# A fused graph network and LSTM kernel: first layer reassociated, first loads reordered, edge tables moved into LSTM pass 2

## The reference, cut to what matters

```python
# x (128 batches, 128 nodes, 128 features), adj (128, 128)
h = relu(einsum('ts,bsh->bth', adj, x @ Wg0 + bg0))
h = relu(einsum('ts,bsh->bth', adj, h @ Wg1 + bg1))
for p in 1, 2, 3, 4:                   # an LSTM over windows of p nodes;
    h[last node of each window] = lstm_last(Wih[p-1], Whh[p-1], ..., windows of p)
x = layernorm(x + h)
x = layernorm(x + edge_attention(x, W_lin, W_val, a, W_out, adj, src, dst))   # 256 edges
```

## Time and profile before

| | us |
|---|---|
| median of 3 runs | 902.23 (901.87 to 903.23) |
| the profiled execution | 902.41 |
| its span in the trace | 900.6 |
| PE busy | 873.2 (97%) |
| DVE busy | 695.8 (77%) |
| ACT busy | 611.2 (68%) |
| POOL busy | 175.7 (20%) |

### The profile page before, as it was taken

The page is one execution under the profiler, slowest core; times in us unless marked ns, Lnnn a source line. Parts: engine busy times, 40 slices in busy tenths (PEclk is TensorE's granted clock), DMA queues, the critical chain, the costliest instruction groups (busy, mean ns, idle before and its releaser), DMA issues.

```text
span 900.6 us, 15429 instructions
## 1 busy us (share of the span) xinstructions
PE 873.2 (97%) x5411; PEld 759.2 (84%) x5411; DVE 695.8 (77%) x1570; ACT 611.2 (68%) x1115; POOL 175.7 (20%) x498
## 2 busy tenths in 40 slices
PE   6999999998999999999999999999998999999996
PEld 6888888886787779999998887878887888888885
DVE  5777777777778777777777676767987887887886
ACT  1777777776777676677667666666787676776354
POOL 0000000000000000000000010003465465566765
PEclk9999999999999999999999999999999999999999
DMA  4212221001000000000000067677155011110222
GB/s 112 78 43 57 71 60 47 25 1 47 1 1 0 1 1 1 1 1 1 1 2 0 1 146 175 147 170 158 48 116 119 14 36 37 36 37 24 58 62 82
DMA packets 43275, 45.44 MB, mean 50 GB/s; under 512 B 2592, under 2 KB 40128, under 8 KB 40128
## 3 DMA queue, kind: packets, MB, share of 16 engines
q1 hardware_dynamic: 39520, 27.47, 10.6%
q0 software_dynamic: 2304, 16.78, 9.2%
q10 hardware_dynamic: 1376, 0.22, 0.2%
HBM read 19.29 MB, written 8.39 MB: 31 GB/s over the span
## 4 chain that ended last, share of the span: by engine, by line
PE 85%; DVE 8%; ACT 3%; issue 2%; POOL 0%; POOLq 0%; DVEq 0%; ACTq 0%
PE psum L446 8%; PE psum L448 8%; PE psum L447 8%; PE psum L464 6%; PE psum L460 6%; PE psum L461 6%; PE psum L1102 6%; PE psum L1178 6%; PE psum L364 3%; PE psum L382 3%; PE psum L392 3%; PE psum L1191 2%; PE psum L1158 2%; PE psum L355 2%; PE psum L354 2%
## 5 line engine op out<-in xcount | busy, mean ns | idle before, releaser
L564 ACT ACTIVATE work<-psum,bias 128x512 f32<-128x512 f32 (+1 forms) x408 | 233.1, 622 | 29.2 <-PE psum L464 28.6
L446 PE MATMUL psum<-hT_hi,w_hi 128*128 128x512 f32 (+1 forms) x408 | 148.8, 365 | 3.3 <-ACT work L564 2.6
L448 PE MATMUL psum<-hT_hi,w_lo 128*128 128x512 f32 (+1 forms) x408 | 147.3, 361 | 0.0
L447 PE MATMUL psum<-hT_lo,w_hi 128*128 128x512 f32 (+1 forms) x408 | 147.3, 361 | 0.0
L548 ACT ACTIVATE work<-work 128x512 f32<-128x512 f32 (+1 forms) x112 | 63.8, 570 | 102.3 <-DVE work L819 70.9
L1010 POOL DMA_DIRECT2D hT_lo<-hT_hi x8 | 7.3, 916 | 556.9 <-DVE hT_lo L794 537.7
L828 DVE TENSOR_TENSOR work<-work 128x512 f32<-128x512 f32 (+1 forms) x111 | 67.8, 611 | 54.1 <-ACT work L548 54.1
L460 PE MATMUL psum<-hs_hi,w_hi 128*128 128x512 f32 (+1 forms) x288 | 103.8, 360 | 0.8 <-DVE hs_hi L792 0.6
L464 PE MATMUL psum<-hs_lo,w_hi 128*128 128x512 f32 (+1 forms) x288 | 104.3, 362 | 0.0
L461 PE MATMUL psum<-hs_hi,w_lo 128*128 128x512 f32 (+1 forms) x288 | 103.2, 358 | 0.0
L446 PEld LDWEIGHTS psum<-hT_hi,w_hi 128*128 128x128 f32 x408 | 76.8, 188 | 17.4 <-ACT work L564 5.4
(11 more groups left out here) (206 smaller groups left out, 1861.0 us busy)
## 6 DMA issues: line engine op xcount, KB each, us to landing
work<-x SPq DMA_DIRECT2D x32, 256.0 KB, 3.0
x_stage<-x_by_feature SPq DMA_DIRECT2D x8, 1024.0 KB, 5.6
hT_lo<-hT_hi POOLq DMA_DIRECT2D x8, 1024.0 KB, 9.7
hT_lo<-x_stage POOLq DMA_DIRECT2D x8, 1024.0 KB, 7.0
out<-x_kept SPq DMA_DIRECT2D x31, 256.0 KB, 2.3
work<-L_gnn_Wih SPq DMA_DIRECT2D x4, 256.0 KB, 3.5
work<-L_gnn_Whh SPq DMA_DIRECT2D x3, 256.0 KB, 3.0
out<-x_kept SPq DMA_DIRECT2D x2, 128.0 KB, 2.3
```

What stands on the lines that cost most here:

```text
L446: pe.matmul(out, w_hi[:, w, g, :], xh, start=True, stop=False)
L447: pe.matmul(out, w_hi[:, w, g, :], xl, start=False, stop=False)
L448: mm = pe.matmul(out, w_lo[:, w, g, :], xh, start=False, stop=(t == 0))
L564: op = act.activation(gate[s][g][:, 0:ph.width], psum[:, 4 * s + g, 0:ph.width], ACT.Tanh if g == G else ACT.Sigmoid, bias=bias[:, b:b + 1])
```

## The change

Eight things are done.

1. First layer. Per tile PE computes `xw` = x times Wg0 first (four fp32 products, from a host-side layout `xb` with features on the partitions), ACT writes its high part, DVE a new low part (`xw_ready`), and `h1` = adj times xw is three F32R matmuls of 512 columns instead of four fp32 products. `adjT` is split once for it.
2. First loads. x is loaded from `xb` in rows of 2048 bytes. SP issues x tile 0, waits until it has landed, and only then issues tiles 1 and 2, the weights, the edge numbers and `a`. ACT issues Wg0, adj and the bias first, then runs a one-column activation, then the rest.
3. PE runs five small matmuls on `ones` before adj is there, and one after its transpose.
4. `degrees` moves behind slot 0, `rank_rows` behind slot 1, the LSTM biases get their own transposition behind slot 3.
5. The attention's weights are centred after slot 6, turned after slot 7 and copied after slot 8.
6. The edge tables leave pass 1: on DVE they go before items 1, 3, 5, 7, 8, 12, 13, 15, 16, 17, 19 and 21 of pass 2, on PE before items 8, 12 and 16 of pass 2 (`sort_cols`, `sort_rows` in F32R, `adjacent`, in bank F) and item 6 of pass 3 (`log_to_rows`), on ACT the logarithm goes behind item 2 of pass 3.
7. In the last slots of pass 1 ACT reads gate O before it does tanh, DVE does the cell product earlier, and in slot 36 PE does the I and G products of pass 2's item 0 ahead of the last O product.
8. `region_free` also waits for `log_ready`.

```diff
 # run_sync
-        sp.dma_start(adj_sb[:, :], adj).then_inc(S["adj_loaded"], 16)
         load_x(0)
-        sp.dma_start(wg0[:, :], Wg0).then_inc(S["wg0_loaded"], 16)
-        sp.dma_start(edge_row_i[:, :], ...)
+        sp.wait_ge(x_loaded[0], 16)
         load_x(1)
+        load_x(2)
         load_piece(0)
         for j, w in enumerate((W_lin, W_val, W_out)):
             sp.dma_start(w_raw[1][:, j, :], w).then_inc(raw_loaded[1], 16)
-        load_x(2)
+        sp.dma_start(edge_row_i[:, :], ...)
+        for j, e in enumerate((src, dst)):
+            sp.dma_start(edge_col_i[:, j, :], ...)
+        sp.wait_ge(S["a_zero"], 1)
+        for h in range(HEADS):
+            sp.dma_start(T.a_wide[...], ...)
 # run_scalar, before its first activation (src, dst and a go to SP)
+        act.dma_start(wg0[:, :], Wg0).then_inc(S["wg0_loaded"], 16)
+        act.dma_start(adj_sb[:, :], adj).then_inc(S["adj_loaded"], 16)
         act.dma_start(bg0_all[:, :], ...)
+        act.wait_ge(S["consts"], 1)
+        act.activation(first_act[:, :], ones[:, 0:1], ACT.Copy)
         act.dma_start(bg0_col[:, :], ...)
         act.dma_start(wg1[:, :], Wg1).then_inc(S["wg1_loaded"], 16)
 # run_tensor, slot
-                    mm = pe.matmul(psum[:, AX, b * P:(b + 1) * P], x_tile[n % X_RING][:, b, :], adjT[:, :], start=True, stop=True)
-                mm.then_inc(S["ax_psum"], 1)
+                    mm = pe.matmul(psum[:, XW, b * P:(b + 1) * P], x_tile[n % X_RING][:, b, :], wg0[:, :], start=True, stop=True)
+                mm.then_inc(S["xw_psum"], 1)
...
-                for b in range(BT):
-                    mm = pe.matmul(psum[:, H1, b * P:(b + 1) * P], axT[k % 2][:, b * P:(b + 1) * P], wg0[:, :], start=True, stop=True)
-                mm.then_inc(S["h1_psum"], 1)
+                pe.wait_ge(S["xw_ready"], k + 1)
+                out = psum[:, H1, :]
+                pe.matmul(out, adjT_hi[:, :], xw_hi[:, k % 2], start=True, stop=False)
+                pe.matmul(out, adjT_lo[:, :], xw_hi[:, k % 2], start=False, stop=False)
+                pe.matmul(out, adjT_hi[:, :], xw_lo[:, k % 2], start=False, stop=True).then_inc(S["h1_psum"], 1)
...
+            if n - 5 == tiles - 1:
+                first_input(I, XW, S["xw_ready"])
+                first_input(G, AH, S["ahT_ready"])
             if has(n - 5):
                 gate_product(O, n - 5)
...
+        pe.wait_ge(S["consts"], 1)
+        run_warm(5)
         pe.wait_ge(S["adj_loaded"], 16)
         pe.wait_ge(S["ident_ready"], 1)
         pe.transpose(psum[:, SIDE, 0:P], adj_sb[:, :], ident[:, :]).then_inc(S["adjT_psum"], 1)
-        degrees()
+        run_warm(1)
 # run_tensor, passes 2 and 3
+                    if ph is phases[1]:
+                        if j in (SORT_COLS, SORT_ROWS, ADJACENT):       # 8, 12, 16
+                            pe.wait_ge(S["gates_read"], ph.items_before + j + (CREDIT - 1))
+                        if j == SORT_COLS:
+                            sort_cols()
+                        elif j == SORT_COLS + 2:
+                            pe.wait_ge(S["cols_ready"], 1)
...
 # run_scalar, slot (n >= 34) and pass 3
+                ended = not has(n - 2)
+                if ended:
+                    gate_of(O, k)
                 act.activation(tanh_c[1], cell[1], ACT.Tanh).then_inc(S["tanh_ready"], 1)
...
+                    if ph is phases[2] and it == 0 and k == LOG_AT:      # 2
+                        act.wait_ge(S["eps_done"], 1)
+                        act.activation(log_adj[:, :], adj_edge[:, :], ACT.Ln).then_inc(S["log_done"], 1)
 # run_vector, slot, between the state's split and h1
+            if has(n):
+                dve.wait_ge(S["xw_hi"], n + 1)
+                dve.tensor_tensor(xw_lo[:, n % 2], psum[:, XW, :], xw_hi[:, n % 2].bitcast(F32), ALU.subtract).then_inc(S["xw_ready"], 1)
 # region_free
+        engine.wait_ge(FS["log_ready"], 1)
```

More of the change, by code:

```diff
@@ L189, in front @@
     CREDIT = 2
-    AX, H1, AH, H2 = range(4)
+    XW, H1, AH, H2 = range(4)
     GATE_BANK = {I: 4, G: 5, O: 6}
@@ L356, in gate_product, with first_input @@
             pe.matmul(out, w_lo[:, 0, g, :], hT_hi[:, cols], start=False, stop=True).then_inc(gate_psum[g], 1)
+        def first_input(g, bank, free):
+            assert bank == g
+            ph = phases[1]
+            pe.wait_ge(free, tiles)
+            pe.wait_ge(S["tiles_done"], ph.batches // BT + CREDIT)
+            xh, xl = windows_at(ph, hi_bt, 0, 0, 0), windows_at(ph, lo_bt, 0, 0, 0)
+            w, out = piece_of[1, 0], psum[:, bank, 0:ph.width]
+            pe.wait_ge(S["w_lo_ready"], len(pieces))
+            pe.matmul(out, w_hi[:, w, g, :], xh, start=True, stop=False)
+            pe.matmul(out, w_hi[:, w, g, :], xl, start=False, stop=False)
+            pe.matmul(out, w_lo[:, w, g, :], xh, start=False, stop=True).then_inc(gate_psum[g], 1)
         def slot(n):
@@ L375, in slot @@
                 k = n - 1
-                pe.wait_ge(S["axT_ready"], k + 1)
                 if k:
@@ L409, in slot, with run_warm @@
                 pe.matmul(out, wg1_lo[:, :], hT_hi[:, cols], start=False, stop=True).then_inc(S["h2_psum"], 1)
+        def run_warm(count):
+            for _ in range(count):
+                pe.matmul(psum[:, GATE_BANK[O], 0:P], ones[:, :], ones[:, :], start=True, stop=True)
+        pe.wait_ge(S["consts"], 1)
+        run_warm(5)
         pe.wait_ge(S["adj_loaded"], 16)
@@ L443, in from_input @@
                     w = piece_of[ph.p - 1, 0]
-                    for g in ((I, G, O) if t == 0 else (F, I, G, O)):
+                    first = ph is phases[1] and it == 0 and k == 0
+                    for g in ((O,) if first else (I, G, O) if t == 0 else (F, I, G, O)):
                         out = psum[:, 4 * (k % 2) + g, 0:ph.width]
@@ L532, in slot @@
                 act.activation(tanh_c[1], cell[1], ACT.Tanh).then_inc(S["tanh_ready"], 1)
-                gate_of(O, k)
+                if not ended:
+                    gate_of(O, k)
         for n in range(SLOTS):
             slot(n)
-            if n == 4:
-                act.wait_ge(S["eps_done"], 1)
-                act.activation(log_adj[:, :], adj_edge[:, :], ACT.Ln).then_inc(S["log_done"], 1)
             if n in piece_slot:
@@ L617, in rank_edges, with spreads_of, edge_keys @@
             dve.tensor_copy(index[:, :], index_i[:, :]).then_inc(S["tables_f"], 1)
+        def spreads_of(j):
+            for c in range(EC):
+                dve.tensor_scalar(spread[:, j, c, :], ones[:, :], edge_col[:, c, j:j + 1], None, ALU.mult).then_inc(S["spreads"], 1)
+        def edge_keys():
             dve.wait_ge(S["tables_f"], 2)
@@ L648, in sorted_edges, with sorted_rows, row_edges, edge_ends @@
             op.then_inc(S["onehots"], 1)
-        def ends_and_sames():
+        def sorted_rows():
+            dve.wait_ge(S["rows_psum"], 1)
+            dve.tensor_copy(sorted_row_r[:, :, :], psum[:, F, :].rearrange("p (j e) -> p j e", j=2)).then_inc(S["rows_ready"], 1)
+        def row_edges():
+            dve.wait_ge(S["rows_ready"], 1)
+            for j in range(2):
+                dve.tensor_scalar(at_node_r[:, j, :], sorted_row[:, j, :], index[:, 0:1], None, ALU.is_equal).then_inc(S["row_edges"], 1)
+        def edge_ends():
             dve.wait_ge(S["row_edges"], 2)
@@ L737, in slot @@
                                   neg_bias[:, :].unsqueeze(1).broadcast_to([P, BT, P]), ALU.max).then_inc(S["h1_ready"], 1)
-            if has(n - 5):
-                k = n - 5
-                dve.wait_ge(S["ig_ready"], k + 1)
-                if k:
-                    dve.wait_ge(S["tanh_ready"], k)
-                dve.tensor_tensor(cell[1], gate[1][I], gate[1][G], ALU.mult).then_inc(S["c_ready"], 1)
+            if has(n - 5) and not ended:
+                cell_product(n - 5)
             if has(n - 2):
```

268 lines of the change are left out of this document (165 added, 103 removed).

## The result

| | before | after |
|---|---|---|
| median of the runs | 902.43 (4 runs, 901.87 to 903.23) | 893.98 (4 runs, 893.92 to 894.24) |
| ratio | | 0.9908, 95% interval 0.9893 to 0.9924 |
| span of the profiled execution | 900.6 | 891.9 |

The change makes the kernel 8.45 us faster. The span falls by 8.7 us, and the two traces, laid side by side, say where. A stage ends where the same instruction starts in both; "first product" is DVE's product of gates I and G of an item. Items are counted from the start of pass 2, which has 32, so item 32 is the first of pass 3.

The account below looks back on a forecast made before the run. PE, busy 97%, was taken to bound pass 1, but not the startup. Gains of 16.4 less costs of 4.9 gave -11.5 on 902.41: 890.9, or 890.7 on the median; 8-in-10 range 886.8 to 896.5, forecast's own 888 to 894.

Parts of the forecast that it names:

- Startup: Start to slot 5's x product: new load and layer order brings it from 30.17 to 22.2, 8.0 gained, bounds 4.7 and 10.2.
- Rival (b): Startup: the loads hold slot 5 to 27, through chained landings and slot 3's x tile; 895.5, chance 0.06.
- the signs of being wrong: Slot over 5.7; PE waiting for DVE in pass 1 or x tile 1 or 3; PE waits over 2 us in pass 2.
- Steady slots: Pass 1, slots 5 to 31: h1 in F32R cuts PE's slot from 5.73 to 5.53, 5.4 gained, bounds 0 and 6.8.
- DVE over 90% busy: Sign of being right: DVE's busy share from 50 to 100 us in pass 1, with PE without waits.
- with 0.5 us of slack per slot: Pass 1, slots 6 and 8: DVE's slack absorbs centring and copying the attention weights (1.8 and 0.6 us), so cost 0.
- The LSTM weight pieces cost the same in both: Pass 1: slots with LSTM weight pieces cost no more after the change than before, so no term for them.
- rival (e): Pass 1: DVE takes over, its new 0.69 comes on top, 6.42 per slot, 18.6 instead of -5.4; 914.7, chance 0.05.
- End of pass 1: Slot 32 to pass 2: gate O before tanh and early products gain 2.7, bounds 1.0 and 3.8; slot 32's h1 another 0.2.
- Pass 2: Edge tables moved here cost PE 2.0, plus 0.9 of DVE stalls before items 8 and 16, bounds 0 and 4.
- Pass 3: Logarithm's table loads on ACT, 2.76 less 1.21 idle, cost 1.5, bounds 0 and 2.8; `log_to_rows` on PE costs 0.5.
- rival (a): Pass 1: slot stays at 5.73, held by the loop through ACT's gates and DVE; 896.3, chance 0.15.

Follow-up runs that it names:

- e10: Changed kernel with LSTM weight pieces cut one slot later, logarithm in pass 4, and DVE's new low part ahead of the state's split: 891.96 us, ratio 0.988.
- e1: Changed kernel with h1 back as four fp32 products and no low part of xw on DVE: 896.66 us, ratio 0.9938.
- e4: Changed kernel with the old end of pass 1, tanh before gate O and no I and G products ahead: 896.73 us, ratio 0.9943.
- e2: Changed kernel with a copy in place of the logarithm in pass 3, so no table load there: 893.21 us, ratio 0.9903.
- e7: Changed kernel with DVE cutting LSTM weight pieces 1 to 6 one slot later, behind the new low part: 894.33 us, ratio 0.9912.

## Why the prediction was right, and where its steps were not

**Startup, 8.0 forecast, 8.27 measured.** Slots 0 to 2 were forecast at 5.2, 8.6 and 11.4 and started at 4.81, 8.25 and 10.91. It is right by its steps but one: `rank_rows` was to wait for the bias row until 10.7, and didn't. The prediction took 6.1 for that row, which is the landing of `bg_col`; PE had waited for `bg_all` (5.4), and both now land in about 3.5. In part the 8.27 is luck: in the next execution that I traced it is 6.55. Rival (b) is out. That slot 1 waits for x tile 1 was in the forecast's own layout, so its place among the signs of being wrong was a slip.

**Steady slots, 5.5 forecast, 4.55 measured.** PE's own share was put too low: with PE busy throughout, the stage is 151.72 (e10), a gain of 6.1. DVE took back 1.6 of it. The slot is 5.50 (5.53 forecast), PE has no waits from 50 to 100 us, and the second of DVE's two waits, 0.73 for gate G, was filled as the step said. The sign "DVE over 90% busy" failed: it is 84%, which by itself would say that there is room. What failed is "with 0.5 us of slack per slot". The 0.5 was slot minus load. But DVE's first wait, 0.53 in the earlier trace rows, is a latency that an added instruction can't use; it grew to 0.73, and DVE's load of 4.75 with it is 5.48 of 5.50. "The LSTM weight pieces cost the same in both" fell with it: with a piece, three slots cost DVE 0.53 more than PE, over six pieces 3.2 us. e1 finds 3.8, the 6.4 of PE's share less the 2.6 that arrived. PE's tolerance hid a part of it in the slots, and it came due at the end. So rival (e) named the mechanism, DVE in order and its waits hanging on ACT, but put the whole 0.69 on top where one of two waits could be filled: 18.6 + 5.4 us in place of some 3.5.

**End of pass 1, 2.7 and 0.2 forecast, 0.72 measured.** The mechanism is right, by e4 2.55. DVE's lateness lands here, 1.8 of it, and 0.8 more in e10.

**Pass 2, 2.9 forecast, 2.81 measured.** The 0.9 of stalls in that sum is not what its parts give: 0.2 and 0.4, and as much again, are 1.2. In the trace PE waits 0.30 near item 10, as foretold, and 0.40 for `adj_done`, one of the three waits that were put at nothing. That the sum fits is in part luck. PE's edge tables are near their prices; the answers to the earlier trace rows in the timeline of PE:

```profile
224.96 1.02 PE L337 MATMUL psum<-edge_col,permute 128*128 128x2 f32 x8
...
242.16 0.63 PE L345 MATMUL psum<-permute,spread 128*128 128x256 f32 x4
```

From start to start they take 0.89 and 0.47, where 0.8 with 0.09 of border and 0.5 were forecast.

**Pass 3, 2.0 forecast, 2.35 measured.** The table loads take 2.03 (e2) where I had 1.5, that is 2.76 less a wait of ACT of 1.21; of the 2.81 that ACT was away only 0.8 was covered. That wait ended with DVE, so it too may have been a latency and no slack, which no run tests. The forecast also had no term for a wait for `log_ready`, where PE stood 0.62. `log_to_rows` took 0.3, not 0.5. A table load lasts 1.28, and what follows it starts 0.01 or 0.02 later: 331.79 to 333.09, and 333.31 to 334.60. The Trainium skill (ScalarE: Activation LUTs, "What ACT_TABLE_LOAD costs") puts 2.66 us on a switch with a drain; the trace disagrees, and the sum by that rule, 893.3, is near the measured 894.0 only because pass 1 gained less.

Sum: forecast 11.5, measured 8.7. Missing are 3.1 in the two stages of pass 1 and 0.35 in pass 3; 0.7 came on top in the startup, in pass 2 and at the end. So 893.98 lies 3.3 above the forecast of 890.7, well inside the range of 886.8 to 896.5 but at the very edge of the forecast's own 888 to 894. It is nearer to rival (a), 896.3, whose cause didn't come about, as the slot fell to 5.50.

## What to carry to other kernels

Before you give an engine one more instruction per round, split its idle time into waits that shrink when it is late (for PE's pace) and latencies that it pays each round (its own result, through another engine, back to it). Busy time plus these latencies is its shortest round, and that is what to hold against the bound engine's slot, the rare longer slots included. If it is within some hundredths, moving an instruction pays where it shortens the round (e7, 6.52 to 6.40); where it doesn't (e10), it moves only the place where the bound engine waits.

Work that no one needs soon (here the logarithm) is placed where the engine that does it has slack, pass 4 and not pass 3, and its price is then 0.35 to 0.5 and not 2.35.

The rows point to one more step, which was not tried: ACT is idle 1.66 before the tanh while PE's O product is done at 140.44. Reading gate O before the tanh in all slots, as the change does for the last ones, would let DVE start at about 142.9 and not 143.49, an estimate. In the last slots, where this is done and DVE's cell product stands earlier too, L827 at 190.06 and at 193.19 shows no wait, but at 196.44 it shows 0.84.

## What the runs showed of the hardware

- The same program runs its first matmuls at half speed, up to a time that differs by some 4 us between executions, between 8 and 13 us (1.16 or 2.07 for the group at 8.3). This moves the end by up to 1.7 us. The granted clock reads 1.00 all the while. The spread is larger than the effects of the hold (0.45), of the rows (0.3) and of the later cut (0.69).
- From slot 5 on, three executions of the changed kernel agree within 0.02 us per stage up to pass 3.
- In the first 32 us the x tiles of 256 KB land in 2.9 us (median) with rows of 2 KB and in 3.1 with rows of 512 bytes, against 4.0 before. The 0.5 KB load lands in 3.5, in 5.3 without the hold, and took 6.1 before.
- A table load of ACT lasts 1.28 us, and the next function starts 0.01 or 0.02 behind it.
